# An attention and LoRA block in fp32 on one core: modulation vectors computed slice by slice in the opening, and the first query tile's scores in two matmuls

## The chip, the cores and the metric

The kernel runs on one core of a Trainium2 chip. The metric is device time in microseconds (us) for one execution, the median of three runs. The core has TensorE (PE; its weight loads are PEld), VectorE (DVE), ScalarE (ACT), GpSimd (POOL) and SyncE (SP), which here only issues DMAs.

## The reference, cut to what matters

Four sequences of 512 tokens, width 1024. A vector c per sequence gives six modulation vectors, and a block of attention and one of mixed LoRA experts follow.

```python
mod = (silu(c) @ wmod).reshape(4, 6, 1, -1)          # wmod: 1024 x 6144
sa, ca, ga, sb, cb, gb = (mod[:, i] for i in range(6))
ga = (2 * (ga >= 0) - 1) * maximum(abs(ga), 0.25)    # gb the same
h = layernorm(x) * (1 + ca) + sa
x = x + ga * attention(h)    # 32 query heads, 8 KV heads of 128, rope, causal window of 256
h = layernorm(x) * (1 + cb) + sb
x = x + gb * experts(h)      # top 2 of 8 experts, rank 64
```

## The kernel before

All products keep fp32 accuracy by splitting an operand into a high part (`_hi`, fp32r) and the rest (`_lo`): `mm3` (L674) issues three matmuls, weights x moving: hi x hi, hi x lo and lo x hi (L675 to L677). h is kept turned, `hT`, with the 1024 features in 8 chunks k of 128 partitions.

The work is 4 sequences x 8 KV heads = 32 groups n. A group projects K, Q0 to Q3 (4 query heads share a KV head) and V, applies rope, and runs 16 units u of attention: query tile i = u // 4 (128 queries), head u % 4. A unit is scores (`pe_scores`, L724), mask and row maximum in one VectorE instruction (`dve_mask`, L1131), exp on ScalarE (L909), normalisation (L1146), a turn of the probabilities by transposes (`pe_turn`, L740), a split on ScalarE (L1003) and VectorE (L1166), and the product with V (L751). Scores of tile 0 need 128 keys, but the matmul is issued with 256 columns (`FAST_N`). Every engine follows an order written out by hand; semaphores tie them together. Between the turns of most groups TensorE does the K products of the next group; groups 7, 15, 23 and 31 end a sequence and have none at their first turns.

The opening, `p0_*`, does group 0's projections and what comes before them.
- SP (`p0_sp`, L139) loads c, the identity, w_k, and then the first 2048 columns of `wmod` (shift and scale of the first block) in 8 pieces of 128 rows, 1 MB each, into four buffers. Then come pieces of w_q (loads 0 to 3), the rope tables, w_v (load 4), the rows of `wmod` for the gate ga (`gate_slice`, 8 slices of 512 KB, four buffers in `acc`), and loads 5 to 9: w_k of the next group and four pieces of w_o. Loads use two `stage` buffers in turn: load j waits for the split of an earlier one (`first_load`, L126). ScalarE's queue loads x in four tiles (L1020).
- TensorE (`p0_pe`, L269) multiplies each piece as it comes ("row k", L277): silu(c), turned, is the weight, 32 columns wide, and the four quarters of the 2048 columns go to four 32-partition strips of one bank. After the 8th piece ScalarE copies the bank (L165), TensorE turns it by four transposes (L284), and VectorE writes `modT` and `modcur` (L226, L1216). Only then can a chunk of h be made: transposes of the normalised x (`pe_ln_chunk`, L833), scale and shift on ScalarE (L1034), high part (L1037), low part on VectorE (L1229). TensorE then adds chunk k to K in bank 0 and to Q0 in bank 1, 6 matmuls a chunk.
- After chunk 7 the rope of K starts on ScalarE (L891, L892) and VectorE (L1099, L1100, L1103), while TensorE runs gate slices 0 to 3 (L251). Q1 goes to bank 0 and waits until the rope has read it (L1100). Slices 4 and 5 follow Q1, 6 and 7 follow chunk 3 of Q2.
- Between ropes ScalarE makes high parts of the loaded weights (L626) and VectorE low parts (L644, L650). After rope 2 VectorE makes the gate row `mrow` (`dve_late_gate`, L185, L190 to L198), which SP stores in four pieces (L182). Before rope 4 VectorE waits for these stores, because `mrow` lies in the memory that `prob` takes:

```python
            for r in range(1 + GQ):
                ...
                if r == GQ:
                    eng.wait_ge(s_md[0], 64)
                dve_rope(eng, 0, r, split=True)
                if r == 2:
                    dve_late_gate(eng, 0, mrow[:], mabs[:], msgn[:])
```

- Rope 4 (`dve_rope`, L1089) begins with the masks of units 0 and 1 and the low part of w_o's last piece, and ends with mask 2, the normalisation of units 0 and 1 and Q3's low part (L1115). TensorE meanwhile does scores 0 and 1, V, with scores 2 after V's fifth chunk, and then turn 0 (L740).
- SP: a gate slice i of 4 or more waits until slice i-4 has been multiplied (`s_mm1`), and what is queued behind it waits too; load 7 comes after slice 7.

## Time and profile before

| | |
|---|---|
| Time, median of 3 runs | 2623.61 us (2623.1 to 2626.34) |
| The profiled execution, its own time | 2622.87 us |
| Its span, first to last instruction | 2621.1 us |
| PE busy | 2585.9 us, 99% |
| PEld busy | 2151.6 us, 82% |
| DVE busy | 1587.9 us, 61% |
| ACT busy | 1156.8 us, 44% |
| HBM traffic | 190 GB/s over the span |

Times in a profile are microseconds from the first instruction. A row of a timeline gives start, duration, engine, line, operation, output <- inputs, and in brackets the engine's idle time before it and what ended it. Matmuls are pipelined, so the duration of one is longer than the step from one to the next; the work is read from the steps between starts.

### The profile page before, as it was taken

What the parts mean: (1) busy time and instruction counts of PE and PEld (TensorE: products, weight loads), DVE (VectorE), ACT (ScalarE), POOL (GpSimd) and SP (SyncE); (2) the same over time, 40 slices, a digit from 0 to 9 for tenths busy, and PEclk for the clock granted to TensorE, in tenths of its full rate; (3) what the DMA queues carried; (4) which work ended last, traced back from release to release, by engine and by line L of the source; (5) the groups of instructions that cost most, each with busy time, mean ns of one, the idle gap of its engine ahead of it and who ended that gap; (6) DMA issues with size and microseconds to landing.
All of it is one profiled execution on the core that took longest, in us unless ns stands there. A gap on an engine that the chain in (4) does not pass through costs nothing.

```text
span 2621.1 us, 40239 instructions
## 1 busy us (share of the span) xinstructions
PE 2585.9 (99%) x12873; PEld 2151.6 (82%) x12873; DVE 1587.9 (61%) x4192; ACT 1156.8 (44%) x2579; POOL 156.4 (6%) x82
## 2 busy tenths in 40 slices
PE   7999999999999999999999999999999999999999
PEld 3888888887888888888888888888888888887887
DVE  6676776666665665556666565556666655546543
ACT  4566665453455443333445443333434443335441
POOL 0211122220000000000000000000000000000122
PEclk9999999999999999999999999999999999999999
DMA  8756776648445453337434454337454556546221
GB/s 325 262 208 248 252 265 241 225 165 340 176 146 183 176 185 141 116 141 281 172 137 168 176 185 160 122 137 279 169 200 178 206 193 225 189 166 256 97 81 57
DMA packets 156312, 499.78 MB, mean 191 GB/s; under 512 B 15088, under 2 KB 39984, under 8 KB 154672
## 3 DMA queue, kind: packets, MB, share of 16 engines
q1 hardware_dynamic: 151744, 482.23, 50.3%
q10 hardware_dynamic: 4464, 16.25, 1.6%
q8 instruction: 54, 0.88, 0.1%
q14 instruction: 50, 0.41, 0.0%
HBM read 376.76 MB, written 121.67 MB: 190 GB/s over the span
## 4 chain that ended last, share of the span: by engine, by line
PE 75%; issue 18%; POOL 3%; DMA 2%; DVE 2%; ACT 0%; ACTq 0%; SPq 0%; POOLq 0%; DVEq 0%
PE bank L675 23%; PE bank L677 23%; PE bank L676 23%; PE bank L740 4%; POOL w_q_lo L631 2%; DMA wm<-in_wmod 1%; POOL w_v_lo L631 1%; DMA ga_t<-mod_scratch 1%; PE bank L251 1%; PE bank L1670 1%; DMA stage<-in_wo 0%; PE bank L766 0%; DVE acc L1330 0%; PE bank L696 0%; PE bank L1711 0%
## 5 line engine op out<-in xcount | busy, mean ns | idle before, releaser
L675 PE MATMUL bank<-w_o_hi,qo_hi 128*128 128x512 f32 x1024 | 411.3, 402 | 0.8 <-DVE acc L1123 0.7
L675 PE MATMUL bank<-hT_hi,w_q_hi 128*128 128x512 f32 x1024 | 400.9, 392 | 2.6 <-DVE swapped L1100 2.6
L677 PE MATMUL bank<-w_o_hi,qo_lo 128*128 128x512 f32 x1024 | 400.3, 391 | 0.0
L676 PE MATMUL bank<-w_o_lo,qo_hi 128*128 128x512 f32 x1024 | 399.0, 390 | 0.0
L676 PE MATMUL bank<-hT_lo,w_q_hi 128*128 128x512 f32 x1024 | 398.6, 389 | 0.0
L677 PE MATMUL bank<-hT_hi,w_q_lo 128*128 128x512 f32 x1024 | 398.5, 389 | 0.0
L1136 DVE CUSTOM_DVE_ANT_0 prob<-bank,mask_t 128x384 f32<-128x384 f32 (+2 forms) x512 | 232.0, 454 | 151.7 <-PE bank L677 93.5
L909 ACT ACTIVATE prob<-prob,nbias 128x384 f32<-128x384 f32 (+2 forms) x512 | 273.5, 534 | 114.1 <-DVE nbias L1136 101.2
L1003 ACT ACTIVATE pT_hi<-bank 128x384 fp32r<-128x384 f32 (+2 forms) x512 | 204.6, 406 | 235.2 <-PE bank L740 229.0
L1099 DVE TENSOR_TENSOR rotated<-bank,cos_t 128x512 f32<-128x512 f32 x160 | 110.6, 691 | 293.7 <-ACT swapped L892 291.5
L1123 DVE TENSOR_TENSOR acc<-bank,acc 128x512 f32<-128x512 f32 x256 | 173.7, 689 | 176.1 <-PE bank L677 176.0
L1166 DVE TENSOR_TENSOR pT_lo<-bank,pT_hi 128x384 fp32r<-128x384 f32 (+2 forms) x512 | 229.6, 448 | 75.2 <-ACT pT_hi L1003 60.7
L891 ACT ACTIVATE swapped<-bank 64x512 f32<-64x512 f32 x160 | 95.3, 596 | 341.5 <-PE bank L677 326.0
L675 PEld LDWEIGHTS bank<-hT_hi,w_q_hi 128*128 128x128 f32 x1024 | 192.2, 188 | 46.3 <-DVE swapped L1100 4.9
L677 PEld LDWEIGHTS bank<-w_o_hi,qo_lo 128*128 128x128 f32 x1024 | 192.2, 188 | 41.9
L677 PEld LDWEIGHTS bank<-hT_hi,w_q_lo 128*128 128x128 f32 x1024 | 192.2, 188 | 40.2
L676 PEld LDWEIGHTS bank<-hT_lo,w_q_hi 128*128 128x128 f32 x1024 | 192.3, 188 | 39.0
L675 PEld LDWEIGHTS bank<-w_o_hi,qo_hi 128*128 128x128 f32 x1024 | 192.4, 188 | 37.8 <-DVE qo_lo L1128 0.9
L676 PEld LDWEIGHTS bank<-w_o_lo,qo_hi 128*128 128x128 f32 x1024 | 192.8, 188 | 36.6
L740 PE MATMUL bank<-ident_t,prob 128*128 128x128 f32 x1152 | 205.3, 273 | 7.9 <-DVE prob L1146 7.5
L1146 DVE TENSOR_SCALAR prob<-prob,rrow 128x384 f32<-128x384 f32 (+2 forms) x512 | 183.0, 363 | 0.3
L740 PEld LDWEIGHTS bank<-ident_t,prob 128*128 128x128 f32 x1152 | 149.9, 140 | 32.1 <-DVE prob L1146 12.7
(211 smaller groups left out, 4540.8 us busy)
## 6 DMA issues: line engine op xcount, KB each, us to landing
w_q_hi<-w_q_hi_scratch SPq DMA_DIRECT2D x96, 512.0 KB, 8.4
w_q_lo<-w_q_lo_scratch SPq DMA_DIRECT2D x96, 512.0 KB, 8.9
w_o_hi<-w_o_hi_scratch SPq DMA_DIRECT2D x96, 512.0 KB, 7.9
w_o_lo<-w_o_lo_scratch SPq DMA_DIRECT2D x96, 512.0 KB, 8.6
stage<-in_wq SPq DMA_DIRECT2D x32, 512.0 KB, 6.0
stage<-in_wo SPq DMA_DIRECT2D x32, 512.0 KB, 5.1
w_q_hi_scratch<-w_q_hi SPq DMA_DIRECT2D x32, 512.0 KB, 6.4
w_q_lo_scratch<-w_q_lo SPq DMA_DIRECT2D x32, 512.0 KB, 7.0
```

The source lines that it names most:

```text
L675: eng.matmul(o, st[0], mv_[0], start=start, stop=False)
L676: eng.matmul(o, st[0], mv_[1], start=False, stop=False)
L677: return eng.matmul(o, st[1], mv_[0], start=False, stop=stop)
L740: m = eng.transpose(bank[5 + u % 2][:, b * P:(b + 1) * P], prob[:, u % GQ, b * P:(b + 1) * P], ident_t[:])
L891: eng.activation(swapped[slot][0:half, :], bk[half:HD, :], ACT.Copy)
L909: eng.activation(tile, tile, ACT.Exp, bias=nbias[:, u:u + 1], scale=-1.0, accum_out=rowsum[:, u:u + 1]).then_inc(s_exp, 1)
L1003: eng.activation(pT[i % 2][0][:, 0:nk, h * P:(h + 1) * P], bank[5 + u % 2][:, 0:nk * P].rearrange("p (b q) -> p b q", q=P), ACT.Copy).then ...
L1099: eng.tensor_tensor(rotated[slot][:], bk[:], cos_t[:], ALU.mult).then_inc(s_dve, 1)
L1123: eng.tensor_tensor(a, wo_bank(half)[:], a, ALU.add).then_inc(s_wor, 1)
L1136: plain(eng.tensor_tensor_reduce(prob[:, u % GQ, 0:w], SBANK[u % 3][:, 0:w], mask_t[:, 3 * P - w:3 * P], -SCALE, FAR, ALU.add, ALU.min, nb ...
L1146: plain(eng.tensor_scalar(tile, tile, rrow[:, u:u + 1], None, ALU.mult)).then_inc(s_nrm[u % GQ], 1)
L1166: eng.tensor_tensor(lo, bank[5 + u % 2][:, 0:nk * P].rearrange("p (b q) -> p b q", q=P), hi.bitcast(F32), ALU.subtract).then_inc(s_ptl, 1)
```

## The change

There are two parts.

**The opening by columns.** The 2048 columns of `wmod` are reordered ahead of the run. Piece i = (q, z) now holds, for 256 shift columns and 256 scale columns (those of chunks 2q and 2q+1), the rows of half z of the 1024, four row tiles side by side. So pieces 2q and 2q+1 complete two chunks. A row adds four row tiles in four strips of a bank; `pe_open_turn` multiplies the copied bank by `sel`, a 128x4 matrix that sums the strips and turns them in one step, four columns at a time into bank 6. VectorE writes `modT` for the two chunks, and ScalarE reads it directly. TensorE's order for q is: row 2q, product of chunk 2q-2, transposes of chunks 2q and 2q+1, row 2q+1, turn q, product of chunk 2q-1. SP's `wmod` loads wait for the second x tile, and loads 0 to 3 stand between the pieces. Gate slices 0 to 3 move from before Q1 to after it, 4 and 5 to after chunk 3 of Q2, 6 and 7 to after Q2; the gate row moves from behind rope 2 to behind rope 3.

**The first tile's scores.** `kt_hi` and `kt_lo` become one tensor `kt_all` of nine tiles, the ninth zero. Two matmuls give [q_hi k_hi + q_lo k_hi | q_hi k_lo + 0] in 256 columns, and VectorE adds the second half to the mask before the reduction.

```diff
         def p0_sp(eng):
             ...
-            for k in range(KT):
-                if k >= 4:
-                    eng.wait_ge(s_mm0, k - 3)
-                eng.dma_start(wm[k % 4][:], wmod[k * P:(k + 1) * P, 0:2 * D]).then_inc(s_wm[k % 4], 16)
-            for j in (0, 1):
-                first_load(eng, j)
+            eng.wait_ge(s_xb[1], 16)
+            for i in range(KT):
+                if i >= 4:
+                    eng.wait_ge(s_mm0, i - 3)
+                eng.dma_start(wm[i % 4][:], wmod[i * P:(i + 1) * P, 0:2 * D]).then_inc(s_wm[i % 4], 16)
+                if i % 2 == 1:
+                    first_load(eng, i // 2)
         def p0_act(eng):
             ...
+            for q in range(4):
+                eng.wait_ge(s_mm0, 2 * q + 2)
+                if q >= 2:
+                    eng.wait_ge(s_mt0, q - 1)
+                eng.activation(swapped[q % 2][:], bank[SLICES[q % 2]][:], ACT.Copy).then_inc(s_mr0, 1)
+                eng.wait_ge(s_mod0, 2 * q + 2)
+                for k in (2 * q, 2 * q + 1):
+                    act_ln_chunk(eng, k, LNB[k % 3])
         def p0_dve(eng):
             ...
+            for q in range(4):
+                dve_first_hi(eng, q)
+                eng.wait_ge(s_mt0, q + 1)
+                for s in range(2):
+                    dst = modT[0][:, :, s, 2 * q:2 * q + 2].rearrange("p b c -> p c b")
+                    at = (2 * q + s) * 2 * BATCH
+                    src = bank[6][:, at:at + 2 * BATCH].rearrange("p (c b) -> p c b", b=BATCH)
+                    eng.tensor_scalar(dst, src, float(s), None, ALU.add).then_inc(s_mod0, 1)
+                if q == 0:
+                    eng.wait_ge(s_split, 2)
+                dve_first_lo(eng, q)
+                for k in (2 * q, 2 * q + 1):
+                    dve_ln_chunk(eng, 0, k)
             ...
-                if r == 2:
+                if r == 3:
                     dve_late_gate(eng, 0, mrow[:], mabs[:], msgn[:])
+        def pe_open_row(eng, i):
+            q, z = divmod(i, 2)
+            if z == 0 and q >= 2:
+                eng.wait_ge(s_mr0, q - 1)
+            eng.wait_ge(s_wm[i % 4], 16 * (i // 4 + 1))
+            for j in range(4):
+                m = eng.matmul(bank[SLICES[q % 2]][32 * j:32 * j + 32, :], cT[:, 4 * z + j, :], wm[i % 4][:, j * 512:(j + 1) * 512],
+                               start=z == 0, stop=z == 1)
+            m.then_inc(s_mm0, 1)
+        def pe_open_turn(eng, q):
+            if q == 0:
+                eng.wait_ge(s_sel, 3)
+            else:
+                eng.wait_ge(s_mod0, 2 * q)
+            eng.wait_ge(s_mr0, q + 1)
+            for cc in range(4):
+                at = (4 * q + cc) * BATCH
+                m = eng.matmul(bank[6][:, at:at + BATCH], swapped[q % 2][:, cc * P:(cc + 1) * P], sel[:], start=True, stop=True)
+            m.then_inc(s_mt0, 1)
         def p0_pe(eng):
             ...
+            for q in range(4):
+                pe_open_row(eng, 2 * q)
+                if q:
+                    pe_open_chunk(eng, 2 * q - 2)
+                for k in (2 * q, 2 * q + 1):
+                    pe_ln_chunk(eng, 0, k, LNB[k % 3], 3)
+                pe_open_row(eng, 2 * q + 1)
+                pe_open_turn(eng, q)
+                if q:
+                    pe_open_chunk(eng, 2 * q - 1)
+            for k in (KT - 2, KT - 1):
+                pe_open_chunk(eng, k)
             for h in range(1, GQ):
                 def gate(k, h=h):
-                    for i in {(1, 7): (4, 5), (2, 3): (6, 7)}.get((h, k), ()):
+                    for i in {(1, 7): (0, 1, 2, 3), (2, 3): (4, 5), (2, 7): (6, 7)}.get((h, k), ()):
                         pe_gate_slice(eng, i)
         def pe_scores(eng, n, u):
             ...
-            cols = max(P * len(kts), FAST_N)
+            cols = P * len(kts)
+            if i == 0:
+                q_hi, q_lo = sl(qo, lambda q: q[:, h, 0:P])
+                pair = SBANK[u % 3][:, 0:2 * P].rearrange("p (z k) -> p z k", k=P)
+                eng.matmul(pair, q_hi, kt_all[:, 0:QT + 1:QT, :], start=True, stop=False)
+                eng.matmul(pair, q_lo, kt_all[:, 0:2 * QT + 1:2 * QT, :], start=False, stop=True).then_inc(s_S, 1)
+                return
         def dve_mask(eng, n, u):
             ...
+            add = mask_t[:, 3 * P - w:3 * P]
+            if u < GQ:
+                add = prob[:, u, 0:P]
+                eng.tensor_tensor(add, SBANK[u % 3][:, P:2 * P], mask_t[:, 2 * P:3 * P], ALU.add).then_inc(s_m0, 1)
+                eng.wait_ge(s_m0, GQ * n + u + 1)
```

## Rows read from the trace of the kernel before

**Rows 1.** The page, parts 1 and 2: busy time, and the granted clock in tenths.
```profile
PE 2585.9 (99%) x12873; PEld 2151.6 (82%) x12873; DVE 1587.9 (61%) x4192; ACT 1156.8 (44%) x2579; POOL 156.4 (6%) x82
...
PEclk9999999999999999999999999999999999999999
```

**Rows 2.** Waits of TensorE: who waited for whom, us in total, times, longest.
```profile
PE bank L277 <- DMA wm<-in_wmod: 10.5, 8, 5.9
PE bank L740 <- DVE prob L1146: 7.5, 11, 1.8
```

**Rows 3.** Busy time of a stretch (last columns clock, DMA share, GB/s); timeline of the opening.
```profile
26.00:28.00 2.00, 1.17 (x12) 0.47 (x12) 0.00 (x0) 0.00 (x0) 0.00 (x0) 1.00 1.01 422
...
12.53 1.94 PE L277 MATMUL bank<-wm,cT 128*32 128x512 f32 x8 [5.93 <-DMA wm<-in_wmod]
...
18.31 2.98 DVE L1225 TENSOR_SCALAR xb<-xb,lnv 128x1024 f32<-128x1024 f32 x4
...
24.90 1.07 PE L277 MATMUL bank<-wm,cT 128*32 128x512 f32 x8 [0.71 <-DMA wm<-in_wmod]
...
29.89 1.06 PE L277 MATMUL bank<-wm,cT 128*32 128x512 f32 x8 [0.85 <-DMA wm<-in_wmod]
31.02 0.60 ACT L165 ACTIVATE swapped<-bank 128x512 f32<-128x512 f32 x1 [14.15 <-PE bank L277]
...
33.10 0.78 ACT L1034 ACTIVATE rotated<-bank,modcur 128x512 f32<-128x512 f32 x1 [0.54 <-DVE modcur L1216]
...
34.57 0.69 DVE L1229 TENSOR_TENSOR hT_lo<-rotated,hT_hi 128x512 fp32r<-128x512 f32 x1 [0.44 <-ACT hT_hi L1037]
...
35.90 0.47 PE L675 MATMUL bank<-hT_hi,w_k_hi 128*128 128x512 f32 x1
```

**Rows 4.** Timeline from K's last matmul to Q1's first.
```profile
47.22 0.39 PE L677 MATMUL bank<-hT_hi,w_k_lo 128*128 128x512 f32 x1
...
48.22 2.09 PE L251 MATMUL bank<-acc,cT 128*32 128x256 f32 x32
...
50.32 0.50 PE L675 MATMUL bank<-hT_hi,w_q_hi 128*128 128x512 f32 x1
```

**Rows 5.** Timeline: the first turn of group 0.
```profile
75.92 0.27 PE L740 MATMUL bank<-ident_t,prob 128*128 128x128 f32 x1
```

**Rows 6.** Timeline: scores of units 0 and 1 of group 13, first matmul of each three.
```profile
1026.45 0.28 PE L675 MATMUL bank<-kt__hi,qo_hi 128*128 128x256 f32 x1
...
1026.80 0.28 PE L675 MATMUL bank<-kt__hi,qo_hi 128*128 128x256 f32 x1
```

**Rows 7.** VectorE's groups by form: busy us, mean ns, idle before.
```profile
L1166 DVE TENSOR_TENSOR pT_lo<-bank,pT_hi 128x128 fp32r<-128x128 f32 x128 | 35.4, 276 | 2.5 <-ACT pT_hi L1003 1.9
```

**Rows 8.** Timeline of group 13: normalisation of units 0 and 1, and turn 0.
```profile
1031.47 0.48 DVE L1146 TENSOR_SCALAR prob<-prob,rrow 128x128 f32<-128x128 f32 x2
...
1033.02 0.28 PE L740 MATMUL bank<-ident_t,prob 128*128 128x128 f32 x1
```

**Rows 9.** Timeline: turn 0 of group 1.
```profile
151.47 0.33 PE L740 MATMUL bank<-ident_t,prob 128*128 128x128 f32 x1 [1.75 <-DVE prob L1146]
```

**Rows 10.** Timeline: small fp32 matmuls of the second block.
```profile
2410.22 0.94 PE L1700 MATMUL bank<-iota_t,lgT 16*128 16x8 f32 x7
```

**Rows 11.** Timeline of SP's queue: gate slices 4 to 7, and loads 7 to 9.
```profile
48.92 2.03 SPq L137 DMA_DIRECT2D acc<-in_wmod  x4
53.90 8.83 SPq L414 DMA_DIRECT2D stage<-in_wo  x3
```

**Rows 12.** Timeline: load 7's high part, the gate's first instruction, its stores.
```profile
60.06 1.06 ACT L626 ACTIVATE w_o_hi<-stage 128x1024 fp32r<-128x1024 f32 x1 [1.27 <-DMA stage<-in_wo]
...
62.90 0.42 DVE L190 TENSOR_SCALAR mabs<-bank 128x256 f32<-128x256 f32 x1
...
65.74 1.32 SPq L182 DMA_DIRECT2D mod_scratch<-mrow  x4
```

**Rows 13.** DMA issues up to 60 us: KB each, median us from issue to landing.
```profile
stage<-in_wv SPq DMA_DIRECT2D x1, 512.0 KB, 3.6
```

108 lines of the change are left out of this document (42 added, 66 removed).

## The prediction

> **What bounds the kernel now.** The page comes first: TensorE is busy in 99% of the span, and its clock is granted in full [rows 1]. So only two kinds of time can be won, work taken off TensorE and the little time in which it waits. The waits of TensorE show where that is: 10.5 us for `wmod` in the opening, 7.5 us in 11 places for normalised probabilities, the longest 1.8 [rows 2]. The timeline of the opening then shows what ends each wait. The eight pieces of `wmod` arrive 2.49 us apart, the DMA engines full (share 1.01, 422 GB/s), and the first product of h comes only at 35.90, after the last piece at 29.89 [rows 3]. From there to 48.3 TensorE is nearly full. The K projection's last matmul starts at 47.22, and Q1, which needs the bank that the rope of K reads, starts at 50.32, 3.10 us later; four slices of the gate's product (2.09 us) fill that gap [rows 4]. The last landmark is the first turn (L740) of group 0, at 75.92, for which TensorE does not wait [rows 5].
>
> The sum is made against the profiled execution: 2622.87 us, of which 2621.1 are span. The median of the runs shown is 2623.61, 0.74 above it, so I add 0.74 at the end. A measurement of this kernel can tell about 0.2% from no change, 5.25 us.
>
> **Part A: the first query tile's scores.** Three matmuls of 256 columns become two, of the same width, since the 256 columns are now two blocks of 128 from two places. Three take 0.35 us from start to start [rows 6], so one is 0.118 us. There are 4 such units in each of 32 groups: 128 x 0.118 = 15.1 us less on TensorE. The read in two blocks has no row here; I take the same 0.118, for the columns are as many. Its bounds are 0 and 0.118 extra for each of the 256 matmuls that stay, up to +30 us.
>
> VectorE gets an addition of 128x128 from PSUM, and a wait for its own result before the reduction. The nearest row, L1166 with 128x128, takes 0.276 us [rows 7]; with the wait I take 0.31, bounds half and double of the row. This is free where the turns have slack. I compared the end of each L1146 with the start of the L740 that uses it, group by group, at the first turns.
> - In 20 groups (8 to 14, 17 to 22, 24 to 30) the smallest slack is 0.67 to 0.9 us; turn 0 of such a group stands in [rows 8]: the first of the two L1146 ends at 1031.76, 1.26 before the turn. The addition fits, and 4 x 0.118 = 0.47 is won: -9.4.
> - In groups 1 to 6 turn 0 already comes right on VectorE (slack 0.05 to 0.32; group 1 stalls 1.75 us [rows 9]). There the addition before unit 2's mask delays turn 0 by up to 0.31, the matmuls taken away before it win nothing, and only unit 3's 0.118 is left: -0.06 to +0.2 each, +0.7 in sum.
> - Groups 7, 15, 23 and 31 have no K products between the first turns, and TensorE waits twice in each (8 of the 11 places). The chain starts at unit 3's scores: -0.47 + 0.31 = -0.16 for three of them. Group 7 also waits for unit 3's query, which comes after unit 2's addition: +0.55. Group 16, with slack 0.05 at its third turn: -0.2. In sum -0.1.
> - Group 0 after its first turn: -0.1.
>
> Part A is -8.9 us behind 75.92.
>
> **Part B: the opening.** (1) `wmod` now waits for the second x tile. The bytes are the same and full engines carried them before, so the first two pieces land as before, at 12.5 and 15.0. x lands sooner: its normalisation started at 18.31 and takes 2.98 [rows 3], because the last tile's statistics began only at 14.8. Three small additions for `sel` (0.6) and four statistics of 1.5 us, now without a wait, end it 2.9 us earlier: x is normal at 18.4 instead of 21.3.
> (2) Row 0 runs at 12.5. Row 1 stands behind the transposes of chunks 0 and 1, which need x: 18.4, eight transposes (0.95 us at full rate, up to twice that after the idle time; I take 1.6), then a row at 1.94, since the first rows took 1.94 us where later ones took 1.07 [rows 3]: 22.0. The copy of `swapped` adds 0.65 [rows 3] and the turn 1.05: it is eight matmuls with 128 weight columns and 4 moving ones, and seven such with 8 moving ones take 0.94 us [rows 10]. Lower bound 0.66, the four old transposes. Here the Trainium skill (TensorE: Matmul & The Clock Gate, LDWEIGHTS) says that a weight load costs by its columns, whatever its rows; by that the price of L1700, with 16 rows, holds for 128, and no run here shows it. Turn 0 of the opening ends at 23.7.
> (3) From the end of a turn to its first product: modT 0.3, identity and copy 1.47, subtraction and hand-over 0.85, 2.6 us [rows 3]. Meanwhile the second product of the slice before (1.37) and a row (1.0) run. Then a product 1.37, eight transposes 0.94, a row 1.12, the copy 0.65, the turn 1.05, in this order on one engine. A round takes 7.75 us, more than its pieces need to arrive (2 x 2.49 + 1.24 = 6.2). Three rounds: 47.0. Chunk 6 starts at 49.6, chunk 7 at 51.0, its last K matmul at 51.5: **4.3 us later than the 47.22 of before**. The early start is eaten by the serial rounds.
> (4) Q1 starts 3.1 behind it, 54.6. The four gate slices that filled this gap now stand behind Q1: 2.1 more. TensorE is 6.4 late, less 0.35 from three cheaper scores.
> (5) Slices 4 to 7 wait for slices 0 to 3 to be used, on SP's queue, and w_o's second piece (load 7) is queued behind them. Before, they went at 48.92 and load 7 at 53.90 [rows 11]; ScalarE already waited 1.27 us for it at 60.06 [rows 12]. Now slice 4 goes at 60.7. A lone load of 512 KB lands 3.6 us after its issue [rows 13], 1.24 of it bytes at 422 GB/s and so 2.4 for start and landing; five of them in a row end at 60.7 + 2.4 + 6.2 = 69.3. ScalarE stands there in rope 2, and VectorE with it: 9.2 late.
> (6) From there, with durations of the same stretch: load 7's hi 70.4, its lo 71.6, Q's lo 72.2, rope 3 with w_o's third lo 75.3, its own lo 75.9. Now follows the gate, moved from behind rope 2 to behind rope 3: 2.8 us, from its first instruction to the issue of its stores [rows 12]: 78.7. Before, stores and landing lay under rope 3. Now rope 4 waits for them at once: the last of four is issued 1.0 later [rows 12] and lands 2.4 after that: 82.1.
> (7) Two masks with additions 1.4, w_o's last lo 1.16, rope 1.9, reciprocals 0.2, mask 2 0.7, normalise 0.3: **turn 0 of group 0 at 87.8, 11.9 later than before**. TensorE is ready at 82.0 and waits 5.8.
>
> Later loads and stores of SP slide with it, but the first piece of group 1 was issued at 86 and used past 105. I cost that at nothing; if its cover is gone, ScalarE's first hi of group 1 is late. The zero tile, the spare tile and the reordering of `wmod` ahead of the run cost nothing either: the copy runs while VectorE waits for c.
>
> **Sum:** 2622.87 + 11.9 - 8.9 + 0.74 = 2626.6, 0.11% slower.
>
> **Rivals.** *The clock falls.* The granted clock reads 1.00 everywhere, but the first rows, after six idle microseconds, ran at 1.94 instead of 1.07, so on the lower of the two levels (1.2 and 2.4 GHz), from 12.53 until some time before 24.90 [rows 3]. The wait of 5.8 us in (7) is as long; those of its kind now are 1.8 at most [rows 2]. At half rate for nothing up to those twelve microseconds it costs between 0 and 6; I take 3: 2629.6, slower. The Trainium skill (same page, Why this matters for your kernels) speaks against the change here: idle gaps between bursts of matmuls bring the lower clock back. By it the sum would be this one.
> *The opening pays.* If load 7 and the gate's stores come in time, only the 6.05 us of (4) stand, net 2620.8. If each round is also 1 us shorter, because turns cost their lower bound and rates are full from the start, it is 3 to 4 us less: 2617.3, **faster**. It decides where the last K matmul starts before 48.5 and TensorE waits less than 1 us before the first turn. Against it: the serial order in the code and [rows 11].
> *The two-matmul scores give nothing*, since the read in two blocks costs what it saves: 2635.5. For it I have no row.
> *The change doesn't do what it says*: products wait for the last piece after all. It lands near 34, and chunk 6 comes long after, so I give this nothing.
>
> **Chances.** Forecast as summed 0.45 (most of it within 0.2%), clock 0.27 (half of it beyond), the opening pays 0.18 (a third of it within), scores give nothing 0.10. Faster 0.13, within 0.2% 0.47, slower 0.40. The range takes in the clock and the paying opening: 2618 to 2634.
>
> **What would show it.** Right: modT and products from about 26 us, turns some 7.75 apart; the last L677 of K near 51.5; ScalarE waiting for `stage` from 61 to 69; VectorE waiting for the landing of `mod_scratch` after the gate; TensorE idle 4 to 7 us before the first L740; 128 matmuls fewer with 256 columns, at the same 0.28 us; a group from 8 on 0.47 shorter. Wrong: Q1 before 52, or no wait at the first L740.

## The result, and the profile after

The changed kernel takes **2635.1 us**, median of five executions (2633.59 to 2636.33), against 2623.61 for the kernel before in five of its own (2622.01 to 2626.34). The ratio is 1.0044, with a 95% interval from 1.0033 to 1.0055: slower by 11.5 us. The prediction said 2626.6, range 2618 to 2634. Its sign was right, its size was 8.5 us too small, and the result lies 1.1 us above the range. The profiled execution took 2635.1, with a span of 2633.3, 12.2 more than before.

The page, part 1, answers to [rows 1]:

```profile
PE 2582.2 (98%) x12773; PEld 2145.3 (81%) x12773; DVE 1616.9 (61%) x4328; ACT 1154.7 (44%) x2581; POOL 156.4 (6%) x82
```

TensorE has 100 matmuls fewer: 128 scores less, 28 more in the turns of the opening. It is busy 3.7 us less and the kernel is 11.5 us slower: TensorE's idle time has grown from 35.2 to 51.1 us. Part of the loss is in the busy time too, since work at half rate counts as busy. The waits of TensorE, against [rows 2]:

```profile
PE bank L780 <- DVE prob L1189: 14.7, 18, 4.1
...
PE bank L286 <- DMA wm<-in_wmod: 6.1, 1, 6.1
PE bank L708 <- DVE swapped L1138: 5.8, 3, 2.2
PE bank L873 <- DVE xb L1268: 3.5, 1, 3.5
PE bank L299 <- ACT swapped L169: 3.2, 4, 0.8
PE bank L806 <- ACT swapped L1030: 2.9, 1, 2.9
```

The wait for `wmod` has shrunk from 10.5 to 6.1 us, as intended, but each of the other rows is new or has grown. The timeline of the opening, against [rows 3, 4]:

```profile
18.09 1.97 PE L873 MATMUL bank<-ident_t,xb 128*128 128x128 f32 x8 [3.54 <-DVE xb L1268]
19.98 1.93 PE L286 MATMUL bank<-wm,cT 128*32 128x512 f32 x8
22.73 1.84 PE L299 MATMUL bank<-sel,swapped 128*128 128x4 f32 x8 [0.81 <-ACT swapped L169]
24.50 1.94 PE L286 MATMUL bank<-wm,cT 128*32 128x512 f32 x8
27.11 0.79 PE L708 MATMUL bank<-hT_hi,w_k_hi 128*128 128x512 f32 x1 [0.67 <-DVE hT_lo L1272]
...
32.72 1.03 PE L299 MATMUL bank<-sel,swapped 128*128 128x4 f32 x8 [0.81 <-ACT swapped L169]
...
40.62 1.02 PE L299 MATMUL bank<-sel,swapped 128*128 128x4 f32 x8 [0.81 <-ACT swapped L169]
...
48.52 1.03 PE L299 MATMUL bank<-sel,swapped 128*128 128x4 f32 x8 [0.81 <-ACT swapped L169]
...
54.04 0.39 PE L710 MATMUL bank<-hT_hi,w_k_lo 128*128 128x512 f32 x1
...
57.14 0.73 PE L708 MATMUL bank<-hT_hi,w_q_hi 128*128 128x512 f32 x1 [2.03 <-DVE swapped L1138]
```

The first product of h comes 8.8 us sooner (27.11, not 35.90), and K's last matmul still comes 6.8 us later (54.04, not 47.22). The turns are 9.99, 7.90 and 7.90 us apart. Rows, transposes, turn and product up to 29.8 run at half rate: a turn takes 1.84, and 1.03 from the second on. Then Q1 starts at half rate as well. The windows show the clock there and at the first turn of group 0 (us, busy time of PE, PEld, DVE, ACT and POOL, granted clock, DMA share, GB/s):

```profile
57.00:60.00 3.00, 2.86 (x7) 2.29 (x8) 2.01 (x4) 2.13 (x3) 0.00 (x0) 0.54 0.25 98
60.00:63.00 3.00, 3.00 (x14) 2.35 (x13) 2.66 (x4) 0.83 (x3) 0.00 (x0) 0.89 0.00 0
87.00:91.00 4.00, 0.16 (x2) 0.16 (x2) 3.82 (x12) 1.29 (x5) 0.00 (x0) 1.00 1.02 404
91.00:95.00 4.00, 4.00 (x17) 3.58 (x17) 2.59 (x13) 2.12 (x10) 0.00 (x0) 0.57 1.02 402
```

The rest of the way to the first turn, from the timelines of SP, ScalarE, VectorE and TensorE, against [rows 11, 12, 5]:

```profile
65.14 1.75 SPq L138 DMA_DIRECT2D acc<-in_wmod  x4
...
74.25 1.06 ACT L659 ACTIVATE w_o_hi<-stage 128x1024 fp32r<-128x1024 f32 x1 [8.51 <-DMA stage<-in_wo]
...
83.05 1.33 SPq L186 DMA_DIRECT2D mod_scratch<-mrow  x4
...
85.37 0.29 DVE L1177 TENSOR_TENSOR prob<-bank,mask_t 128x128 f32<-128x128 f32 x1 [2.35 <-DMA mod_scratch<-mrow]
...
90.84 0.33 PE L780 MATMUL bank<-ident_t,prob 128*128 128x128 f32 x1 [4.09 <-DVE prob L1189]
```

Load 7 stops ScalarE for 8.5 us, the stores of the gate row stop VectorE for 2.35, and TensorE, last, waits 4.09 us. Turn 0 of group 0 starts 14.9 us later than before.

For the rest of the span I compared the start of each group's V turn (the four transposes of `swapped`, L766 before, L806 after) with the kernel before, group by group. The first number of a row is how much later the V turn of group 0 comes; the others are by how much that delay changes over the groups named. All are us, from the one profiled execution of each kernel; the time is the median, the ratio that to the kernel before on the same chip, with its interval.

| kernel | time, ratio | g0 | 1-7 | 8 | 9-15 | 16 | 17 | 18-31 |
|---|---|---|---|---|---|---|---|---|
| changed | 2635.1, 1.0044 (1.0033 to 1.0055) | 15.74 | 1.02 | 1.26 | -3.34 | 4.99 | -0.88 | -6.90 |
| scores_only | 2615.42, 0.9969 (0.9956 to 0.9981) | 0.46 | 0.32 | 1.01 | -3.33 | 0.76 | 0.34 | -6.81 |
| opening_only | 2640.03, 1.0066 (1.0053 to 1.0080) | 11.36 | -0.71 | 0.69 | 0.00 | 3.57 | 0.03 | -0.01 |
| slices_back | 2632.98, 1.0037 (1.0023 to 1.0051) | 12.60 | 2.51 | 3.01 | -3.33 | 2.97 | 0.66 | -6.72 |
| slices_gate_back | 2626.7, 1.0013 (1.0004 to 1.0022) | 7.86 | 1.97 | 1.14 | -3.33 | 3.00 | 0.74 | -6.21 |
| row_back | 2631.89, 1.0036 (1.0024 to 1.0048) | 13.22 | -0.41 | -0.15 | -3.33 | 3.01 | 0.58 | -6.78 |
| warm | 2633.94, 1.0037 (1.0024 to 1.0051) | 12.81 | 1.76 | 0.01 | -3.34 | 4.66 | 1.76 | -6.92 |
| after_pad8 | 2633.56, 1.0035 (1.0022 to 1.0047) | 16.53 | 6.03 | 1.01 | -3.33 | 0.07 | -0.04 | -6.67 |
| scores_pad4 | 2617.85, 0.9975 (0.9965 to 0.9986) | -0.61 | 0.84 | 1.10 | -3.34 | 2.98 | 0.62 | -5.99 |
| scores_pad8 | 2620.37, 0.9990 (0.9981 to 0.9999) | -0.46 | 0.61 | 1.13 | -3.33 | 3.64 | 1.63 | -6.77 |
| scores_noadd | 2611.0, 0.9953 (0.9940 to 0.9967) | -0.01 | -2.12 | -0.41 | -3.34 | -0.63 | -0.12 | -6.65 |
| all_repairs | 2619.1, 0.9983 (0.9974 to 0.9992) | 4.72 | 0.61 | 1.46 | -3.33 | 0.70 | -0.38 | -6.00 |
| repairs_order | 2613.63, 0.9966 (0.9954 to 0.9978) | -1.21 | 0.24 | -0.03 | -3.35 | -0.07 | 0.11 | -6.87 |
| order_alone | 2631.61, 1.0027 (1.0017 to 1.0037) | 9.54 | 3.59 | 0.00 | -3.33 | 3.43 | 1.77 | -6.57 |
| order_cold | 2618.99, 0.9981 (0.9971 to 0.9990) | 0.48 | 1.25 | -0.47 | -3.33 | -0.06 | 0.14 | -6.65 |
| best | 2618.26, 0.9980 (0.9971 to 0.9989) | 0.09 | -0.75 | 1.02 | -3.33 | 3.34 | 1.84 | -6.62 |
| combined | 2613.55, 0.9959 (0.9945 to 0.9972) | -0.77 | 0.62 | 0.80 | -3.33 | -0.46 | 0.35 | -6.80 |

Read the first row: 15.7 us are lost by the first V turn, 2.3 more by group 8, then each group wins 0.47 to 0.57 (0.37 to 0.44 in groups 15, 23 and 31), except that group 16 loses 5.0 and group 17 wins 0.9. The two parts of the change stand apart in the next two rows. Where the intervals of two kernels overlap, their times alone do not settle a difference, and the traces have to carry the reading. That holds for warm, slices_back, row_back, after_pad8, order_alone and opening_only beside the changed kernel, for scores_pad4 and scores_noadd beside scores_only, and for all_repairs and order_cold beside repairs_order.

Groups 8 and 17 follow the clock. TensorE waits 1.69 to 3.87 us for the rope at the end of the first sequence in every kernel, and behind that wait the clock fell in some profiled executions and not in others. Here are the changed kernel and the kernel before, whose waits were 2.17 and 2.44 us:

```profile
668.00:672.00 4.00, 4.00 (x12) 3.14 (x11) 2.68 (x4) 1.81 (x4) 1.10 (x1) 0.57 0.04 17
651.00:655.00 4.00, 4.00 (x20) 3.29 (x18) 2.67 (x4) 1.81 (x4) 1.27 (x1) 1.00 0.01 5
```

In the ten executions with a fall there (changed, scores_only, slices_back, slices_gate_back, after_pad8, scores_pad4, scores_pad8, all_repairs, best, combined) group 8 goes from 0.80 to 3.01; in the seven others of the table from -0.47 to 0.69. Group 17 does the same: 0.58 to 1.84 in the eight executions in which the clock fell at the V turn of group 16 (slices_back, slices_gate_back, row_back, warm, scores_pad4, scores_pad8, order_alone, best), and 0.35 or less in the others.

### The profile page after: what moved, and what is told of

Same layout as the page of the kernel before. It is cut to its first block, busy times and chain, and to the rows that moved or that the text cites. A ratio compares the mean times of both kernels' runs of the same rounds, so it can differ in the third digit from the quotient of the medians.

```text
span 2633.3 us, 40267 instructions
## 1 busy us (share of the span) xinstructions
PE 2582.2 (98%) x12773; PEld 2145.3 (81%) x12773; DVE 1616.9 (61%) x4328; ACT 1154.7 (44%) x2581; POOL 156.4 (6%) x82
## 4 chain that ended last, share of the span: by engine, by line
PE 75%; issue 18%; POOL 3%; DVE 2%; DMA 1%; ACT 1%; ACTq 0%; DVEq 0%; POOLq 0%
PE bank L708 22%; PE bank L710 22%; PE bank L709 22%; PE bank L780 4%; POOL w_q_lo L664 2%; DMA ga_t<-mod_scratch 1%; POOL w_v_lo L664 1%; PE bank L1714 1%; PE bank L261 1%; PE bank L769 0%; DMA stage<-in_wo 0%; PE bank L770 0%; DVE acc L1373 0%; PE bank L806 0%; PE bank L729 0%
## 5 line engine op out<-in xcount | busy, mean ns | idle before, releaser
L1179 DVE CUSTOM_DVE_ANT_0 prob<-bank,mask_t 128x384 f32<-128x384 f32 (+1 forms) x384 | 195.8, 510 | 46.7 <-issue 44.6
```

Of the source, the lines that this page charges most:

```text
L1179: plain(eng.tensor_tensor_reduce(prob[:, u % GQ, 0:w], SBANK[u % 3][:, 0:w], add, -SCALE, FAR, ALU.add, ALU.min, nbias[:, u:u + 1])).then_ ...
```

## The experiments

**scores_only**: the kernel before with the two-matmul scores, the zero tile and VectorE's addition. Its diff is the part of the change in `pe_scores`, `dve_mask` and the tensor `kt_all`; p0 keeps its old order.

> The kernel before with the two-matmul scores and VectorE's addition alone; the opening stays as it was. Theory 1 (the prediction's sum of Part A, corrected by the groups of the changed kernel: -0.5 in each of 20 groups, +1.0 in groups 1 to 7, and the +5.0 of group 16 and +1.3 of group 8 belong to the new opening or to the layout of the program): 9 to 10 us faster than before, 2613.5 to 2614.7. Theory 2 (the +5.0 at group 16 and the +1.3 at group 8 come from the scores' part): 3 to 4 us faster, about 2620, with group 16 again 5 us longer. Rival (reading two blocks costs what it saves): no faster than 2623.

Measured: 2615.42, 8.2 us faster. The time is 0.7 us above theory 1's range. Theory 1 holds for group 16, which loses 0.76 here; group 8's loss stays (1.01), so it was not the opening's. The read in two blocks costs nothing that can be seen; two of the changed kernel's groups of matmuls by form (mean in ns after the busy time) show the first and second of the pair, beside 289, 282 and 283 for the three matmuls of the other tiles with 256 columns:

```profile
L769 PE MATMUL bank<-kt_all,qo_hi 128*128 128x256 f32 x128 | 35.4, 288 | 0.5 <-DVE qo_lo L1153 0.5
L770 PE MATMUL bank<-kt_all,qo_lo 128*128 128x256 f32 x128 | 34.8, 283 | 0.0
```

**opening_only**: the changed kernel with the old scores.

```diff
-            cols = P * len(kts)
-            if i == 0:
-                ...
+            cols = max(P * len(kts), FAST_N)
```

> The changed kernel with the scores of the first tile in three matmuls again and without the addition: the new opening alone. Theory 1: turn 0 of group 0 near 91.2 (15 us later than before), and the 5.0 of group 16 stays: 2623.6 + 15.3 + 5 to 6 = about 2644. Theory 2 (group 16's 5 us belong to the scores): 2639. In both the opening costs 15 us and nothing of it is given back later.

Measured: 2640.03, 16.4 us slower than before. Group 16 loses 3.57 here, in the kernel whose scores are the old ones: its loss belongs to the opening's part of the edit, though it comes some 1180 us later. The time is nearer to theory 2's 2639, but not for theory 2's reason: the opening itself cost less. The first turn of group 0 comes at 87.04, not at 91.2 as expected and 3.8 us sooner than in the changed kernel. From the landing of the stores VectorE needs 4.2 us instead of 5.5, without the additions. The other 2.4 us are from the rate. From TensorE's timeline of this execution:

```profile
22.43 1.03 PE L299 MATMUL bank<-sel,swapped 128*128 128x4 f32 x8 [0.82 <-ACT swapped L169]
...
30.33 1.02 PE L299 MATMUL bank<-sel,swapped 128*128 128x4 f32 x8 [0.81 <-ACT swapped L169]
...
51.66 0.40 PE L710 MATMUL bank<-hT_hi,w_k_lo 128*128 128x512 f32 x1
```

With the same instructions up to here as the changed kernel, full rate is back before turn 0. All rounds take 7.90 us, and K's last matmul starts at 51.66; the prediction said 51.5. Five more profiled executions issue the same instructions up to there, and their last K matmul starts at 54.04 (changed), 54.55 (row_back), 54.98 (after_pad8) and 55.59 (slices_back and slices_gate_back, whose first round takes 11.49 and 11.41 us). So how long the half rate lasts differs between executions of one opening, by up to 3.9 us at its end, and this stands in every comparison of first turns below. This execution (2637.91) was the fastest of its kernel's five.

**scores_noadd**: as scores_only, and VectorE's addition left out, so that the product of q_hi and k_lo is missing from the first tile's scores.

> The two-matmul scores with the old opening, without VectorE's addition of the second block (so one of the three products is left out of these scores). Theory 1 (the addition eats the gain in groups 1 to 7 and partly in 15, 23 and 31, and is hidden in the 20 others): groups 1 to 7 win 0.3 to 0.47 each instead of losing 0.3 in sum, groups 15, 23 and 31 0.6 to 0.7 instead of 0.41, the 20 others stay at 0.48 to 0.53; in all 3 to 4.5 us less than the two-matmul scores with it, 2611 to 2612.5. Rival (those groups were limited by something else, a load or the rope's chain): under 1.5 us less.

Measured: 2611.0, 4.4 us less than scores_only, and 2.4 of it in groups 1 to 7. Groups 9 to 15 and 18 to 31 gain what they gained with the addition. So the addition costs only where VectorE is ahead of turn 0 by nothing, and is hidden elsewhere. One part of theory 1 missed: groups 15, 23 and 31 were to win 0.6 to 0.7 and still win 0.36 to 0.44, so the addition is not what holds them back. Some of the 4.4 us is not the addition's: the clock did not fall at group 8 here, as it did in scores_only.

**slices_back** and **slices_gate_back**: gate slices 0 to 3 in front of Q1 again, and in the second the row too.

```diff
+            for i in range(4):
+                pe_gate_slice(eng, i)
             for h in range(1, GQ):
-                    for i in {(1, 7): (0, 1, 2, 3), (2, 3): (4, 5), (2, 7): (6, 7)}.get((h, k), ()):
+                    for i in {(1, 7): (4, 5), (2, 3): (6, 7)}.get((h, k), ()):
```

```diff
-                if r == 3:
+                if r == 2:
                     dve_late_gate(eng, 0, mrow[:], mabs[:], msgn[:])
```

> The changed kernel with gate slices 0 to 3 back in front of Q1 and 4, 5 and 6, 7 at their old places; the gate row stays behind rope 3. Theory 1 (the late slices delay SP's slices 4 to 7 and with them w_o's second piece): slice 4 is issued near 56 instead of 65.14, ScalarE waits for the stage under 1 us instead of 8.5, TensorE is not idle from 54.9 to 57.1 and Q1 starts at full rate, turn 0 of group 0 at 82 to 84 instead of 90.84, in all 7 to 9 us faster than the changed kernel: 2626 to 2628. Rival (the gate row behind rope 3 with its stores sets turn 0 anyway): turn 0 stays at 87 or later, at most 4 us faster.

> As the kernel with the slices back, and the gate row behind rope 2 again. Theory 1 (with the slices early TensorE sets turn 0, and the row's place costs nothing): within 1 us of the kernel with the slices back alone. Rival (the landing of the stores, met by rope 4 at once, costs its 2 to 3 us on the chain to turn 0): 2 to 3 us faster than the slices back alone. In both what is left against the kernel before is the 6 to 7 us of the later K projection, less the scores' gain.

Both main theories missed, and the rivals named the cause. Load 7 came in time as expected (ScalarE waits 0.57 for it, at 67.74), but the first turn moved only from 90.84 to 87.45. Its row in slices_back, then in slices_gate_back:

```profile
87.45 0.33 PE L782 MATMUL bank<-ident_t,prob 128*128 128x128 f32 x1 [3.38 <-DVE prob L1191]
```

```profile
83.88 0.27 PE L782 MATMUL bank<-ident_t,prob 128*128 128x128 f32 x1
```

With the row behind rope 3, VectorE met its stores at once (2.35 us, until 81.98) and TensorE stood 3.38 us; with the row behind rope 2 TensorE did not wait at all. The row's place is worth 6.3 us in time here: 4.7 at the first V turn, of which 3.6 are the later turn 0 and the rest the half rate that followed the wait. The rival had said 2 to 3.

**row_back**: the changed kernel with the second diff alone.

> The changed kernel with the gate row behind rope 2 again, the slices staying late. Theory 1 (the stores' landing, 2.35 us that VectorE stands for, is hidden under rope 3 again, and TensorE's wait ahead of turn 0 shrinks with the fall of the clock behind it): turn 0 2 to 3 us earlier, 2632 to 2633. Rival (with the slices late the row waits for slice 7 itself and holds up rope 3, so the change had to move it): no gain or a loss of 1 us, 2635 to 2636.

Measured: 2631.89, 3.2 us less, within the noise of the two. Turn 0 at 89.08, 1.8 earlier, with a wait of 1.77 and no fall of the clock behind it (1.00 from 90 to 94). So even with the slices late the row was better at its old place. The two moves do more together than apart: slices alone 2.1 us of time, row alone 3.2, both 8.4; in turn 0's start 3.4, 1.8 and 7.0.

**warm**: 28 matmuls more, in TensorE's idle stretches ahead of row 0 and ahead of the first transposes.

```diff
+            for i in range(14):
+                eng.matmul(bank[0][:, 0:P], ident_t[:], ident_t[:], start=True, stop=True)
             for q in range(4):
                 pe_open_row(eng, 2 * q)
+                if q == 0:
+                    for i in range(14):
+                        eng.matmul(bank[0][:, 0:P], ident_t[:], ident_t[:], start=True, stop=True)
```

> The changed kernel with 28 added matmuls of 128 columns (identity by identity, into a bank that the K product clears later): 14 between the transpose of c and row 0, 14 between row 0 and the first transposes, where TensorE was idle. They use nothing and nothing reads them. Theory 1 (the half rate of rows, transposes, turn 0 and the first product is the part of the opening that the prediction's step 2 missed): row 1 near 1.1 instead of 1.93, turn 0 near 1.05 instead of 1.84, turn 1 near 30 instead of 32.72, the last K matmul near 51.5 instead of 54.04, and the time 2.5 to 3 us lower, 2632 to 2632.6. Rival (the rounds wait for pieces or for ScalarE, not for the rate): under 1 us lower. A further fall after the later waits, at Q1 and at turn 0 of group 0, is expected to stay in both.

Measured: row 1 and turn 0 did what theory 1 says, the rest only partly: turn 1 starts at 31.54, K's last matmul at 52.88, and the time is 1.2 us lower, within the noise. From its timeline:

```profile
21.00 1.02 PE L299 MATMUL bank<-sel,swapped 128*128 128x4 f32 x8 [0.81 <-ACT swapped L169]
...
24.57 0.80 PE L713 MATMUL bank<-hT_hi,w_k_hi 128*128 128x512 f32 x1 [1.54 <-DVE hT_lo L1277]
...
31.54 1.02 PE L299 MATMUL bank<-sel,swapped 128*128 128x4 f32 x8 [0.82 <-ACT swapped L169]
```

Row 1 took 1.06 and turn 0 1.02. The first product then waited 1.54 us, and the clock fell in that wait (0.50 from 24 to 28), so that turn 1 won only 1.2. The same wait of 1.54 us in opening_only brought no fall (1.00 from 24 to 28). Turn 0 of group 0 came 3.0 earlier (87.83), since Q1 ran at full rate. Groups 16 and 17 took 2.3 of it back.

**after_pad8, scores_pad4, scores_pad8**: four or eight activations of 32x1 elements more at ScalarE's start, in the changed kernel and in scores_only. They take nothing from the path; they move the rest of ScalarE's program along.

```diff
+            for i in range(8):
+                eng.activation(pad_t[0:32, i:i + 1], c_in[:, 0:1], ACT.Exp, scale=-1.0)
             eng.activation(c_sig[:], c_in[:], ACT.Exp, scale=-1.0).then_inc(s_sig, 1)
```

> The changed kernel with eight 32x1 activations more at ScalarE's start, where it waits for nothing on the path; they shift all that follows in ScalarE's program by eight instructions. In four kernels with the new opening ScalarE stands twice without a releaser at the start of group 16 (2.4 and then 1.6 to 3.0 us), the second time ahead of the copy that the V turn waits for. Theory 1 (the place of the second stand depends on where the program's instructions lie): with eight more it moves ahead or behind, and group 16 is 2 to 4 us shorter, the time 2631 to 2633. Rival (the stand belongs to the work there, whatever the place of the code): group 16 as in the changed kernel, 2635.

> The two-matmul scores with the old opening and four such activations more on ScalarE. Theory 1 (place of the code): the second stand, which now falls on the copy of pT behind the V turn, moves to the copy ahead of it, as in the kernels with the new opening, and group 16 becomes 2 to 4 us longer: 2617.5 to 2619.5. Rival: no change, 2615.4, within 1 us.

> The two-matmul scores with the old opening and eight small activations at ScalarE's start instead of four. Theory 1 (place of the code on ScalarE): as in the changed kernel with eight, the second stand at the start of group 16 is gone, group 16 is 0.5 to 0.7 us shorter than before instead of 0.76 longer, and the time 1 to 2 us lower than without them: 2613.5 to 2614.5. Rival: the stand stays in some place, 2615.4 or, as with four, 2617.9.

scores_pad4 is a hit, after_pad8 one in group 16 (4.9 us shorter) and a miss by 0.6 us in the time, and scores_pad8 a miss that says the same. ScalarE's timeline at the start of group 16, in the changed kernel, where the releaser "issue" means that the profile names none:

```profile
1267.61 0.63 ACT L941 ACTIVATE qo_hi<-rotated 128x512 fp32r<-128x512 f32 x1 [1.46 <-DVE rotated L1141]
1270.67 0.40 ACT L949 ACTIVATE prob<-prob,nbias 128x128 f32<-128x128 f32 x1 [2.42 <-issue]
...
1273.50 0.60 ACT L1030 ACTIVATE swapped<-bank 128x512 f32<-128x512 f32 x1 [2.34 <-issue]
```

in scores_only, where the second stand falls behind the copy for the V turn (L1001):

```profile
1253.07 0.57 ACT L1001 ACTIVATE swapped<-bank 128x512 f32<-128x512 f32 x1
1255.57 0.28 ACT L1014 ACTIVATE pT_hi<-bank 128x128 fp32r<-128x128 f32 x1 [1.93 <-issue]
```

in scores_pad4, where it falls ahead of it:

```profile
1254.80 0.60 ACT L1004 ACTIVATE swapped<-bank 128x512 f32<-128x512 f32 x1 [3.00 <-issue]
```

in scores_pad8, where both stands fall ahead of the first exp (the row names the last semaphore):

```profile
1255.04 0.40 ACT L923 ACTIVATE prob<-prob,nbias 128x128 f32<-128x128 f32 x1 [5.33 <-DVE nbias L1155]
```

and in after_pad8, where ScalarE has neither; its wait behind the copy is for VectorE, which stands itself (second row, from VectorE's timeline):

```profile
1273.30 0.60 ACT L1033 ACTIVATE swapped<-bank 128x512 f32<-128x512 f32 x1 [0.44 <-PE bank L713]
...
1276.61 0.40 ACT L952 ACTIVATE prob<-prob,nbias 128x128 f32<-128x128 f32 x1 [2.55 <-DVE nbias L1182]
...
1275.52 0.17 DVE L1262 COPY modcur<-modT 128x16 f32 x1 [2.20 <-issue]
```

Group 16 goes 0.76, 2.98, 3.64 with 0, 4 and 8 more in the one kernel, and 4.99, 0.07 with 0 and 8 in the other, with the same work. All other executions agree. The kernels with the new opening and no added activations have the same ScalarE program, and group 16 loses 2.97 to 4.99 in the seven of them; the five with eight more (after_pad8, all_repairs, repairs_order, order_cold, combined) go from -0.46 to 0.70. That the place of ScalarE's code decides is shown.

It does not decide all of it. Of the changed kernel's 4.99, 2.94 is TensorE's wait for that copy. Another 1.62 came before it, since the gate row `ga_t` reached VectorE late at the end of group 15, where the kernel before waits 0.45 for it (rows of VectorE and TensorE):

```profile
1239.56 1.23 DVE L1373 TENSOR_TENSOR acc<-acc,ga_t 128x1024 f32<-128x1024 f32 x1 [2.76 <-DMA ga_t<-mod_scratch]
...
1251.78 0.50 PE L708 MATMUL bank<-hT_hi,w_q_hi 128*128 128x512 f32 x1 [1.62 <-DVE swapped L1138]
```

In opening_only no such wait stands before TensorE's V turn, but TensorE itself stands 2.02 us without a releaser, at 1267.30.

What the stand is, the DMA packets tell. Some queues of the profile are marked as carrying instructions. One of them, with packets of 8 KB, carried nothing in the changed kernel from 1216 to 1268, and three packets from 1268.2 to 1273.5: two before 1270.7, where ScalarE's first stand and one of VectorE's (2.29 us, up to 1271.63) lie, and one in ScalarE's second stand. In after_pad8 it carried one, in VectorE's stand (packets, MB, share of the DMA engines):

```profile
q14 instruction: 3, 0.02, 1.5%
q14 instruction: 1, 0.01, 0.5%
```

scores_only has three in its stands, scores_pad4 and scores_pad8 four, and all_repairs, repairs_order and combined one, like after_pad8. So in these traces the stands go with fetches of instructions. The group is the first behind the jump back of the loop over sequences. The Trainium skill (Runtime: NRT & Kernel Launch, Instruction fetch mechanics) says that instructions are fetched ahead in order, in blocks, and that a taken branch whose target is not held stalls the engine until its block has come. By it one stand follows the jump, and a second one where the next block begins soon after the target; the two stands, their packets and their shift agree, but where the blocks begin was not measured. after_pad8 won 1.5 us of time only, within the noise; in its profiled execution groups 1 and 2 lost 4.2. ScalarE got the next group's w_k piece there at 145.56 after a wait of 4.62 us (at 143.00 after 3.09 in the changed kernel) and the last w_o piece at 164.19 (161.00), so loads landed later; why is open.

**all_repairs**: both diffs of slices_gate_back, the matmuls of warm and the eight activations.

> The changed kernel with four repairs together: gate slices 0 to 3 in front of Q1 (and 4 to 7 at their old places), the gate row behind rope 2, the 28 added matmuls in the idle stretches of the opening, eight small activations at ScalarE's start. Theory 1 (the opening loses by separate causes that add up): from the kernel with slices and gate row back, 2626.7, less 2.5 to 3 for the rate in the opening and 2 to 3 for group 16: 2621 to 2622.5; turn 0 of group 0 near 81.3. What is then left against the old opening with the two-matmul scores (2615.4) is 5 to 6 us, the serial rounds. Rival (one of them is hidden behind another): 2624 or more.

Measured: 2619.1, 2 to 3 us better than theory 1. The opening's losses do add up, and the kernel is now faster than before. Turn 0 of group 0 starts at 80.75, still 4.8 us behind before.

**repairs_order**: in addition, one product changes its place in TensorE's order.

```diff
             for q in range(4):
                 pe_open_row(eng, 2 * q)
-                if q:
-                    pe_open_chunk(eng, 2 * q - 2)
                 for k in (2 * q, 2 * q + 1):
                     pe_ln_chunk(eng, 0, k, LNB[k % 3], 3)
                 pe_open_row(eng, 2 * q + 1)
+                if q:
+                    pe_open_chunk(eng, 2 * q - 2)
                 pe_open_turn(eng, q)
```

> As the kernel with the four repairs, and in each round the first product of the slice before stands behind the round's second row instead of in front of the transposes, so that it covers ScalarE's copy of the rows (TensorE stands 0.8 us for it in each round) and its own chunk is ready before it. Theory 1 (a round of 7.9 us is some 7.0 us of work and 0.8 us of that wait): rounds 7.0 to 7.2 us apart, the last K matmul 2 to 2.7 us earlier, the time 2 to 2.7 us lower than with the four repairs. Rival (the product's inputs come later than the place freed, or the pieces set the pace): under 1 us lower.

Measured: 2613.63, 5.5 us lower, twice what theory 1 says. TensorE's timeline:

```profile
21.82 1.02 PE L301 MATMUL bank<-sel,swapped 128*128 128x4 f32 x8 [0.81 <-ACT swapped L171]
22.77 1.06 PE L288 MATMUL bank<-wm,cT 128*32 128x512 f32 x8
23.77 1.09 PE L883 MATMUL bank<-ident_t,xb 128*128 128x128 f32 x8
24.79 1.06 PE L288 MATMUL bank<-wm,cT 128*32 128x512 f32 x8
25.79 0.50 PE L718 MATMUL bank<-hT_hi,w_k_hi 128*128 128x512 f32 x1
...
27.28 0.95 PE L301 MATMUL bank<-sel,swapped 128*128 128x4 f32 x8
```

The turns are 5.46, 6.90 and 6.86 us apart, where all_repairs has 9.28, 7.91 and 7.90. The later rounds give 1.0 each, as expected. The first gives 3.8: transposes and a row that were ready fill the 2.6 us that the chunk takes, and without the wait the clock does not fall. K's last matmul starts at 46.49, 0.7 us earlier than before the change, and turn 0 of group 0 at 74.83.

**order_alone**, **order_cold**: that order in the changed kernel with nothing else, and repairs_order without the added matmuls.

> The changed kernel with one edit: in each round the first product of the slice before stands behind the round's second row. Theory 1 (the product in front of the transposes blocks what is ready: 1.5 us in the first round, 0.8 us for ScalarE's copy and the 0.15 us of weight loads behind it in the later ones, and the rate falls in the first wait): the last K matmul near 49 to 50 instead of 54.04, turn 0 of group 0 near 86.5, 4 to 5 us faster than the changed kernel: 2630 to 2631. Rival (at half rate the opening's rows and turns set the pace, so the order is worth little without the added matmuls): under 2.5 us faster.

> As repairs_order, without the 28 added matmuls. Theory 1 (row 0, the first transposes, row 1, turn 0 and row 2 run at half rate again, and full rate comes back near 28 as in the changed kernel): 3 to 3.5 us later at Q1 and about 3 us slower, 2616 to 2617. Rival (with no wait left in the rounds the rate comes back sooner, near 24): 1.5 to 2 us slower, 2615.5.

order_alone: K's last matmul at 49.73, 4.3 earlier, and turn 0 at 84.77, 6.1 earlier, more than expected, as Q1 ran at full rate. The time is 3.5 us lower, less than theory 1 says; groups 1 to 7 took 2.6 back, and groups 16 and 17 took 1.1. order_cold: row 0 and the first transposes at half rate, but the opening's turn 0 already took 1.02 us at 23.56, and turn 0 of group 0 came 1.7 later than with the matmuls, as the rival says. But this execution (2614.51) was the fastest of ten, and the medians differ by 5.4 us, more than either theory said. The others may have had a longer half rate, like the changed kernel's; none of them has a profile. What the matmuls are worth is left between 1.7 and 5.4.

**best**, **combined**: scores_pad8 and repairs_order with three matmuls and no addition in groups 0 to 7.

> As that kernel, and in the eight groups of the first sequence the scores are computed as before, by three matmuls and without the addition; the two-matmul form is left to groups 8 to 31. Theory 1 (there the addition on VectorE eats what TensorE wins, the sum of groups 1 to 8 with it being +1.3 us): the groups of the first sequence as before, the time 1 to 1.5 us lower than with the two-matmul form everywhere, about 2612.5. Rival (the groups' times there are set by transfers that vary from one execution to the next): no difference beyond 0.5 us.

> As repairs_order, with the scores of the eight groups of the first sequence in three matmuls without the addition, as in best. Theory 1 (what best showed against scores_pad8, 2.1 us, holds here too): 2611.5 to 2612.5, the fastest of all that compute the reference. Rival: with turn 0 1.2 us earlier the transfers of groups 1 to 7 end the waits and nothing is won, 2613.6.

best took 2618.26 (ratio 0.9980, 0.9971 to 0.9989), combined 2613.55 (0.9959, 0.9945 to 0.9972). The medians fall by 2.1 and by 0.1 us, and both pairs of intervals overlap: not shown. **repairs_order and combined are the fastest kernels here that compute the reference**, 9 to 10 us faster than before and 21 faster than the changed kernel; scores_only is 1.8 us behind them, within what this can tell apart.

## Why the prediction was right and wrong

**Part A was right** in its mechanism, and its sum with some luck. It said -8.9, and scores_only is 8.2 faster. It said 0.47 for each of 20 groups; 18 of them give 0.47 to 0.53 there, and groups 8 and 17 do not. It costed the addition at 0.31 us and said that it eats the gain in groups 1 to 7 (+1.25 in sum; 1.02 in the changed kernel, 0.32 in scores_only). The addition takes 288 ns in 128 instances. Too pessimistic were groups 15, 23 and 31 (-0.36, -0.41 and -0.44, not -0.16). Group 8 was read as a regular one with -0.47 and lost 1.26, behind a fall of the clock that came in ten executions and not in the others. The luck is that in scores_only groups 8, 16 and 17 cost 3.3 us more than said and groups 1 to 7, 9 to 15 and 18 to 31 cost 2.1 less. The measured 2635.1 also lies beside the 2635.5 of the rival by which the scores give nothing. That is chance: scores_only refutes that rival.

**Steps (1), (5), (6) and (7) were right in what follows what, and nearly in size.** x was normal at 18.1 (said 18.4). From slice 4's issue to load 7 ScalarE waited until 9.1 us later (said 8.6). The gate took 2.2 us up to the issue of the stores (said 2.8), and from there VectorE stood 2.35. From the landing to turn 0 it was 5.5 us (said 5.7). TensorE stood 4.1 (said 5.8).

**Step (2) failed in the rate.** It took row 1 at half rate, then the turn and what follows at full. It had written "up to twice that after the idle time" for the transposes and then let the rate come back behind row 1, without a row for it. The half rate lasted until 29.8: turn 0 took 1.84 instead of 1.05, the first product 2.7 instead of 1.37 us. So the first round was 9.99 us instead of the 7.75 of **step (3)**, whose other two came out at 7.90, and K's last matmul was 2.5 us later than said. Where the rate came back sooner, in opening_only, both steps held to 0.2 us. Step (3) took the round as work, though, and it is not: repairs_order shows that 1.0 us of each round, and 3.8 of the first, is the order of one product.

**Step (4) failed at Q1.** The gap of 3.1 us came, but it cost more than the 2.1 of the slices: the clock fell in it, and Q1 up to the slices took 7.3 us instead of the 5.67 that it takes at full rate in warm. That is 1.6 us.

The two arrive in full at load 7, which ends its wait at 74.25 where 69.3 was said. Steps (6) and (7) then gave 1.9 back, since the gate, the landing of its stores and the way to turn 0 were each shorter than said, and 3.0 were left at turn 0.

**The clock rival happened**, as well as the forecast. It had a chance of 0.27, but it looked at one wait only, the one before turn 0. There the price was 0.8 us by the V turn and 1.5 by the turn of unit 2 (79.04 before, 95.49 here, against 14.92 late at turn 0), half of the 3 taken. The half rate that it did not look at cost more: 2.5 us in the opening, 1.6 at Q1, and some 1.3 of group 8's 1.7 (the mean of the executions with a fall there less that of the others). With the 1.5 at turn 0 that is some 7 us. The sentence of the Trainium skill weighed there (TensorE: Matmul & The Clock Gate, Why this matters for your kernels) is borne out by the windows above, but the falls behind 1.54 and 2.03 us came in shorter gaps than those it warns of.

**No step had group 16.** The prediction took it as -0.2, the profile shows +4.99: 2.94 for the stand ahead of the V turn's copy, 1.62 for the late gate row. This is the largest single term of the miss. The terms against the prediction, at the landmarks: +3.0 at turn 0, +0.8 behind it, -0.2 in groups 1 to 7, +1.7 in group 8, -0.4 in groups 9 to 15, +5.2 in group 16, -0.4 in group 17, -0.9 behind it; 8.8, against 8.5 in time.

**The range** ended at 2634 because the clock case was its upper end. A case in which a loss appears far from the edit was not among the rivals. In the kernel before ScalarE already stood 2.6 us without a releaser in front of the first exp of group 16, and I had not asked what another program ahead of it would do.

## What to carry to other kernels

Splitting a late input into slices makes each slice's latency a round on the bounding engine, so write that engine's order down and let nothing that waits for the slice stand ahead of anything that is ready; here one such swap was worth 5.5 us in one kernel and 3.5 in another. Moving small work out of a wait uncovers the wait, and a TensorE that stands may come back at half rate, so the price of a gap is more than its length. Where a program has loops, an edit that changes the number of an engine's instructions can move a stall at a loop's jump onto the path or off it, so compare kernels landmark by landmark before a difference far from the edit is explained by the edit. And read the granted clock at each landmark: one wait of 2 us cost nothing in one execution and over 1 us in the next.

## What the runs showed of the hardware

- The clock fell in gaps shorter than I had thought, and not always. Behind the wait of 2.02 or 2.03 us at Q1 the granted clock was 0.54 in the changed kernel (57 to 60) and in opening_only (55 to 58) and 0.70 in row_back (57 to 60), but 1.00 in warm and order_alone. Behind 1.54 us in the opening it was 0.50 in warm and 1.00 in opening_only. Ahead of turn 0 of group 0, waits of 4.09, 3.93, 3.88, 3.87 and 3.38 us were followed by a fall, and those of 2.37 and 1.77 were not. At the end of the first sequence the waits with a fall were 1.99 to 3.87 us and those without 1.69 to 3.02. A fall cost 1.5 to 1.6 us at Q1 and at turn 0.
- The half rate of the opening's start ended before turn 0 in two profiled executions (opening_only, order_cold), at 29.8 in the changed kernel's and at about 33 in slices_back's: 3.9 us of difference at K's last matmul for the same instructions. The clock column reads 1.00 there all the same (27 to 33 of slices_back), so in the opening the durations have to be read: 0.63 us for a matmul of 512 columns, against 0.39.
- The turns with 4 moving columns take 1.03 us for eight matmuls at full rate and 1.84 at half rate. The 1.05 that the prediction took, from weights of 16 rows and 8 moving columns, was right. The Trainium skill's rule that it weighed there (TensorE: Matmul & The Clock Gate, LDWEIGHTS), a weight load costs by its columns whatever its rows, agrees: these weights have 128 rows.
- A moving operand read in two blocks of 128 columns from two places is as fast as one of 256 in a row (288 and 283 ns, beside 289 and 283).
- Behind a loop's jump ScalarE and VectorE stand 1.6 to 3.0 us at a time while packets of an instruction queue arrive. Four instructions more ahead of them move ScalarE's second stand, and with eight more in the new opening ScalarE has none there (one packet, not three).
